# Adding the causal mask of a diagonal score block on VectorE in place of TensorE

## The chip, the cores and the metric

The kernel runs on one core of one Trainium2 chip. The time is the device time of one execution in microseconds, as the median of several runs. A profiled execution on the same core gives the trace from which all rows below are read. In the trace PE is TensorE's matmul side, PEld its weight load, DVE is VectorE, ACT is ScalarE, POOL is GpSimd and SP is SyncE.

## What is computed

The kernel computes one transformer layer on 2 x 1024 tokens of width 512: a token embedding from a hot and a cold table, a LayerNorm, causal attention with 16 heads of width 32, a residual sum, a second LayerNorm, and a mixture of 16 experts (2 per token) with a shared expert. The change touches the attention only. Cut to that:

```python
qkv = jnp.einsum('bsd,od->bso', x, w_project)            # b=2, s=1024, d=512
q, k, v = ...                                            # [b, 16 heads, s, 32]
att = jnp.einsum('bhqd,bhkd->bhqk', q, k) / math.sqrt(HEAD_DIM)
causal = jnp.triu(jnp.ones((s, s), dtype=bool), k=1)
att = jnp.where(causal[None, None, :, :], jnp.float32(-1e9), att)
att = jax.nn.softmax(att, axis=-1)
out = jnp.einsum('bhqk,bhkd->bhqd', att, v)
```

## The kernel before

The program has three stages that follow each other on each engine: the embedding (up to about 136 us of the span), the attention (136.5 to 634 us) and the output projection with the router and the experts (from 634 us). Each engine has an instruction stream written out by hand, and the streams meet only in semaphores.

The attention is cut into 8 **units**: a unit is one batch row b and one group of 4 heads, so that u = 2g + b. A unit has 32 **steps**, n = 0 to 31. Step n handles head h = n % 4 of the query tile i = n // 4, 128 query rows against (i + 1) * 128 keys. Units 1 to 6 run in a loop of three rounds of two units (`Fori`); units 0 and 7 are written out before and after it.

The order on TensorE within step n is: the scores of step n + 1 (`scores`, L492), the turning of the probabilities of step n - 1 (`turn`, L508), a piece of the projection of the next unit (`fill_piece`, L471, in four steps of five from n = 2 on, and not at all in unit 7, which has no next one), and in each step with n % 4 == 2 the product of the probabilities with V for the query tile before (`heads`, L519), followed by the transposition of the reciprocal sums (L531).

`scores` waits until ScalarE's exp of the step two before it is done (L495), because the scores of even and of odd steps share one pair of PSUM banks each. It multiplies with all keys up to the diagonal in pieces of up to 512 columns (L502). Into the piece that holds the diagonal block it then adds the mask with a second product, the identity times `mask_bf` in bf16 (L504), in the same accumulation. `s_S` is counted up behind the last product. Queries are stored with the negative scale, so the scores are negated, the mask is a large positive number above the diagonal, and the row maximum is taken as a minimum.

VectorE's step n (`unit`, L654) is: `row_max` of step n (L632, the reduction L638), in two or three steps of a unit the copy of a projected piece out of bank 7 (`fill_evac`, L460 and L469), the copy of the second half of the turned probabilities of step n - 2 (`copy_turned`, L584, only for i >= 4), the reciprocals of the sums when n % 4 == 0 (L644 and L646), and `normalize` when n % 4 == 3 (L652), which waits for ScalarE's `z_rows`.

ScalarE's step n is: the copy of the first half of the turned probabilities of step n - 2 (L582), the exp of step n with its row sums (L597), at times a projected piece (L456, L467), and the copy of `z_rows` when n % 4 == 3 (L604).

So a step's scores pass through this chain: TensorE scores, VectorE reduction, ScalarE exp, and from there to TensorE's turn of the same step and to the scores two steps on. VectorE's copies of turned probabilities set PSUM banks 4 and 5 free for later turns.

Of the kernel before, what the change touches and what calls it, by code (L numbers as in the profile page):

```python
# [16 lines left out]
ALU = mybir.AluOpType  # L17
# [3 lines left out]
P = 128  # L21
# [40 lines left out]
def build(nc, a, out):  # L62
    ctx = ExitStack()
    with ctx:
        def sb(name, shape, dt=F32, where=ctx):
            return where.enter_context(nc.sbuf_tensor(name, shape, dt))

        def sem(name):
            return ctx.enter_context(nc.semaphore(name))
# [3 lines left out]
        ident_bf = sb("ident_bf", [P, P], BF16)  # L73
        tri_bf = sb("tri_bf", [P, P], BF16)
        ones_bf = sb("ones_bf", [P, P], BF16)
        mask_bf = sb("mask_bf", [P, P], BF16)
# [11 lines left out]
        def bank(i, n=1):  # L88
            return psum[:, i:i + n, :].rearrange("p a n -> p (a n)")
# [64 lines left out]
        q_stack, k_stack, v_unit = [], [], []  # L154
# [139 lines left out]
        s_fdve = sem("projection_copied_by_dve")  # L294
# [2 lines left out]
        s_stack = [sem(f"stacks_loaded{b}") for b in range(BATCH)]  # L297
        s_S = sem("scores_ready")
        s_M = sem("row_max_ready")
        s_E = sem("probs_ready")  # L300
        s_T = sem("probs_turned")
        s_Ca = sem("probsT_copied_by_act")
        s_Cd = sem("probsT_copied_by_dve")
        s_Zr = sem("z_reciprocal_ready")
        s_Z = sem("z_inverse_ready")
        s_PV = sem("heads_summed")
        s_ZR = sem("z_rows_ready")
        s_AT = sem("attnT_ready")
# [42 lines left out]
        HEAD = 16  # L351
        STACKED = 16 * 8 * GH
        STEPS = QT * GH
        FILLS = 6

        def turned_banks(i):
            return 1 if i < 4 else 2
# [9 lines left out]
        def bank_no(i, h, k):  # L367
            return banks.index((i, h, k))

        def copies(e, upto):  # L370

            return sum(copier(*x) == e for x in banks[:upto])

        def wait_bank_free(pe, u, n):

            m = n - 2
            x = banks[m % UB]
            v = u if m >= 0 else u - 1
            e = copier(*x)
            pe.wait_ge(s_Ca if e == "act" else s_Cd, HEAD + v * UCOPY[e] + copies(e, m % UB + 1))  # L380
# [110 lines left out]
        def att_pe(pe):  # L491
            def scores(u, b, n):  # L492
                i, h = n // GH, n % GH

                pe.wait_ge(s_E, HEAD + u * STEPS + n - 1)  # L495
                dst = bank(2 * (n % 2), 2)
                qs = q_stack[b][:, h, i * P:(i + 1) * P]
                for c0 in range(0, (i + 1) * P, 512):

                    c1 = min(max((i + 1) * P, c0 + 256), c0 + 512)  # L500
                    own = c0 <= i * P < c1
                    mm = pe.matmul(dst[:, c0:c1], qs, k_stack[b][:, h, c0:c1], start=True, stop=not own)  # L502
                    if own:
                        mm = pe.matmul(dst[:, i * P:(i + 1) * P], ident_bf[:, :], mask_bf[:, :], start=False,  # L504
                                       stop=True)
                mm.then_inc(s_S, 1)

            def turn(u, n):  # L508
                i, h = n // GH, n % GH
                pe.wait_ge(s_E, HEAD + u * STEPS + n + 1)  # L510
                for k in range(turned_banks(i)):
                    m = bank_no(i, h, k)
                    wait_bank_free(pe, u, m)
                    for j in range(4 * k, min(4 * k + 4, i + 1)):
                        mm = pe.transpose(bank(4 + m % 2)[:, (j - 4 * k) * P:(j - 4 * k + 1) * P],  # L515
                                          probs[n % PSLOTS][:, j * P:(j + 1) * P], ident[:, :])
                    mm.then_inc(s_T, 1)

            def heads(u, b, i):  # L519

                last = bank_no(i, GH - 1, turned_banks(i) - 1) + 1
                for e, s in (("act", s_Ca), ("dve", s_Cd)):
                    pe.wait_ge(s, HEAD + u * UCOPY[e] + copies(e, last))

                pe.wait_ge(s_AT, HEAD + u * QT + i)
                for j in range(i + 1):
                    for h in range(GH):
                        pe.matmul(bank(6)[32 * h:32 * h + 32, 0:P], v_unit[b][:, j, 32 * h:32 * h + 32],  # L528
                                  probsT[i % 2][:, h, j * P:(j + 1) * P], start=(j == 0), stop=(j == i))
                pe.wait_ge(s_Z, HEAD + u * QT + i + 1)  # L530
                pe.transpose(bank(6)[:, P:2 * P], z_inv[:, i % 2, :, :].rearrange("p h d -> p (h d)"),  # L531
                             ident[:, :]).then_inc(s_PV, 1)

            def unit(u, b, g, prev, nxt):

                for n in range(STEPS):
                    if n + 1 < STEPS:
                        scores(u, b, n + 1)
                    elif nxt:
                        first_scores(u + 1, 1 - b, g + b)  # L540
                    if n >= 1:
                        turn(u, n - 1)
                    elif prev:
                        turn(u - 1, STEPS - 1)
                    if nxt and 0 <= (n - 2) // 5 < FILLS and (n - 2) % 5 < KC:
                        fill_piece(pe, u + 1, 1 - b, (n - 2) // 5, (n - 2) % 5, 16 * (g + 1 + b))
                    if n % GH == 2:
                        if n > GH:
                            heads(u, b, n // GH - 1)
                        elif prev:  # L550
                            heads(u - 1, 1 - b, QT - 1)

            def first_scores(u, b, g):

                pe.wait_ge(s_stack[b], STACKED * (g + 1))
                pe.wait_ge(s_fact, HEAD + 3 * u + 3)
                pe.wait_ge(s_fdve, HEAD + 3 * u + 3)
                scores(u, b, 0)

            first_scores(0, 0, 0)  # L560
            unit(0, 0, 0, False, True)
            with pe.Fori(0, GROUPS - 1) as g:
                unit(2 * g + 1, 1, g, True, True)
                unit(2 * g + 2, 0, g + 1, True, True)
            last = 2 * GROUPS - 1
            unit(last, 1, GROUPS - 1, True, False)
            turn(last, STEPS - 1)
            heads(last, 1, QT - 1)
# [62 lines left out]
        def att_dve(dve):  # L631
            def row_max(u, n):  # L632
                i = n // GH
                dve.wait_ge(s_S, HEAD + u * STEPS + n + 1)

                dve.wait_ge(s_E, HEAD + u * STEPS + n - 3)

                dve.tensor_reduce(nmax[:, n % 4:n % 4 + 1], bank(2 * (n % 2), 2)[:, 0:(i + 1) * P], AX.X,  # L638
                                  ALU.min).then_inc(s_M, 1)
# [832 lines left out]

        @block.vector
        def _(dve):
            for s in (s_M, s_Cd, s_Zr, s_Z, s_AT, s_fdve):
                dve.sem_inc(s, HEAD)
            step = Chain(dve, s_dve)
            dve.wait_ge(s_in, 32)
# [225 lines left out]
```

## Time and profile before

| what | value |
|---|---|
| median of 3 runs | 1120.07 us (1119.99 to 1125.67) |
| profiled execution, whole time | 1121.66 us |
| its span in the trace | 1119.7 us |
| TensorE's mean granted clock | 0.968 of full |
| busy: PE, PEld, DVE, ACT, POOL | 90%, 57%, 49%, 45%, 28% |
| attention, 136.5 to 634 us: busy PE, DVE, ACT | 476.2, 293.6, 351.1 of 497.5 us |

The profiled execution's span is 1119.7 us, and about 2 us lie around it (1121.66 in all). The busy shares are means over stages of different kinds. For a change in the attention, what counts is which engine or wait comes last in the attention, step by step, and that is read from the timeline and from the chain of waits.

### The profile page before, as it was taken

To read this page: it belongs to the slowest core of one execution; us is meant where nothing else is said; L and a number is where in the kernel's file an instruction comes from. 1 tells how busy PE (TensorE), PEld (TensorE's weight loads), DVE (VectorE), ACT (ScalarE), POOL (GpSimd) and SP (SyncE) were. 2 spreads that over 40 slices of the span, in tenths; PEclk is the share of its full clock that TensorE was granted. 3 is DMA by queue.
4 is the path that set the end of the run, shared out by engine and by line. 5 is a ranking of instruction groups with operands and counts; after the bars stand their busy time and mean duration, and the time that the engine had idled before them with its cause. 6 is when DMAs were issued, how large, how long until landed. Compare 5 with 4: busy or idle time off the path is not lost.

```text
span 1119.7 us, 22789 instructions
## 1 busy us (share of the span) xinstructions
PE 1003.6 (90%) x6879; PEld 638.8 (57%) x6880; DVE 551.2 (49%) x1422; ACT 499.1 (45%) x1195; POOL 319.0 (28%) x413
## 2 busy tenths in 40 slices
PE   5767699999989999899998899899898998799994
PEld 3323458676765858477676687778543444344441
DVE  7985347465645657365567677578311111111110
ACT  7512177676757777576778422111121222122221
POOL 1077220111102020110202046333144554445542
PEclk9779799999999999899999999899899999999997
DMA  5032733240513333050434111611296448744443
GB/s 199 30 84 84 177 77 79 70 109 11 135 40 76 78 76 87 26 136 13 105 96 144 61 73 57 263 47 48 93 286 186 85 91 239 232 91 84 85 87 43
DMA packets 44571, 114.35 MB, mean 102 GB/s; under 512 B 9332, under 2 KB 11380, under 8 KB 42162
## 3 DMA queue, kind: packets, MB, share of 16 engines
q1 hardware_dynamic: 32146, 87.14, 26.5%
q0 software_dynamic: 12320, 25.90, 12.1%
q8 instruction: 55, 0.90, 0.3%
q14 instruction: 50, 0.41, 0.1%
HBM read 53.03 MB, written 25.17 MB: 70 GB/s over the span
## 4 chain that ended last, share of the span: by engine, by line
PE 53%; DMA 19%; issue 11%; DVE 8%; POOL 4%; ACT 2%; POOLq 1%; DVEq 0%; ACTq 0%
DMA out<-y_sb,out_no 18%; PE psum L515 10%; PE psum L481 7%; PE psum L528 6%; PE psum L502 6%; PE psum L486 5%; PE psum L1200 4%; PE psum L1184 3%; PE psum L1256 2%; PE psum L531 1%; PE psum L504 1%; PE psum L1277 1%; DVE nmax L638 1%; DVE oh_lo L1497 1%; POOL hot_all L1422 1%
## 5 line engine op out<-in xcount | busy, mean ns | idle before, releaser
L638 DVE TENSOR_REDUCE nmax<-psum 128x1 f32<-128x128 f32 (+7 forms) x256 | 192.1, 753 | 79.9 <-PE psum L504 69.3
L597 ACT ACTIVATE probs<-psum,nmax 128x128 f32<-128x128 f32 (+7 forms) x256 | 190.7, 745 | 53.0 <-DVE nmax L638 47.7
L1256 PE MATMUL psum<-attnT,x_T 128*128 x376 | 182.8, 609 | 9.5 <-issue 8.2
L502 PE MATMUL psum<-k_stack,q_stack 128*128 128x512 f32 (+2 forms) x384 | 157.2, 464 | 24.4 <-issue 15.3
L515 PE MATMUL psum<-ident,probs 128*128 128x128 f32 x1152 | 174.9, 278 | 3.8 <-DVE probsT L584 1.4
L1157 DVE COPY x_T<-psum 128x512 f32<-128x512 f32 x47 | 32.5, 692 | 249.8 <-PE psum L1299 249.8
L582 ACT COPY probsT<-psum 128x512 f32<-128x512 f32 (+3 forms) x256 | 129.1, 504 | 55.2 <-PE psum L515 43.5
L481 PE MATMUL psum<-xnT,w_unit 128*128 128x512 f32 x256 | 131.4, 603 | 0.2 <-ACT full L456 0.2
L515 PEld LDWEIGHTS psum<-ident,probs 128*128 128x128 f32 x1152 | 124.5, 142 | 9.1 <-DVE probsT L584 3.8
L428 POOL CAST part_hi<-full 128x512 fp32r<-128x512 f32 x32 | 19.6, 613 | 375.6 <-ACT full L456 267.7
L1256 PEld LDWEIGHTS psum<-attnT,x_T 128*128 128x128 f32 x376 | 66.1, 193 | 87.5 <-issue 87.1
L502 PEld LDWEIGHTS psum<-k_stack,q_stack 128*128 128x128 f32 x384 | 69.1, 202 | 67.0 <-ACT probs L597 33.2
L1335 PE MATMUL psum<-w_dn,gated_T 128*128 x188 | 88.5, 593 | 1.0 <-ACT gated_T L909 1.0
L850 POOL DMA_INDIRECT out<-y_sb,out_no x47 | 75.4, 1604 | 44.4 <-POOL out_no L847 44.4
L940 ACT ACTIVATE y_sb<-psum,slot_w 128x512 f32<-128x512 f32 x47 | 32.3, 687 | 104.3 <-PE psum L1335 100.4
L528 PE MATMUL psum<-probsT,v_unit 128*32 128x128 f32 x2304 | 77.1, 278 | 0.8 <-ACT probsT L582 0.8
L528 PEld LDWEIGHTS psum<-probsT,v_unit 128*32 128x32 f32 x2304 | 59.8, 111 | 27.7 <-ACT probsT L582 19.4
L652 DVE TENSOR_TENSOR attnT<-psum,z_rows 128x128 f32 (+1 forms) x64 | 18.7, 291 | 114.8 <-ACT z_rows L604 114.8
L486 PE MATMUL psum<-w_unit,xnT 128*128 128x128 f32 x512 | 66.7, 275 | 0.3 <-DVE full L460 0.3
L584 DVE COPY probsT<-psum 128x128 f32<-128x128 f32 (+3 forms) x128 | 61.6, 481 | 2.7 <-PE psum L515 2.5
L836 POOL DMA_INDIRECT x_rows<-xn_scratch,rows_no x47 | 50.0, 1065 | 42.5 <-POOL rows_no L833 36.1
L486 PEld LDWEIGHTS psum<-w_unit,xnT 128*128 128x128 f32 x512 | 61.7, 192 | 0.5 <-issue 0.5
(222 smaller groups left out, 1489.3 us busy)
## 6 DMA issues: line engine op xcount, KB each, us to landing
attnT<-in_wgu SPq DMA_DIRECT2D x16, 1024.0 KB, 5.0
q_stack<-part_hi SPq DMA_DIRECT2D x64, 128.0 KB, 2.4
q_stack<-part_lo SPq DMA_DIRECT2D x64, 128.0 KB, 2.4
k_stack<-part_hi SPq DMA_DIRECT2D x64, 128.0 KB, 2.4
k_stack<-part_lo SPq DMA_DIRECT2D x64, 128.0 KB, 2.6
w_dn<-in_wd SPq DMA_DIRECT2D x16, 512.0 KB, 6.2
out<-acc SPq DMA_DIRECT2D x17, 256.0 KB, 2.1
hot_all<-xn SPq DMA_DIRECT2D x4, 1024.0 KB, 8.3
```

The source lines that it names most:

```text
L481: mm = pe.matmul(bank(7), w_unit[:, k, side * P:(side + 1) * P], xnT[:, k, t0:t0 + 512], start=(k == 0), stop=(k == KC - 1), skip_group_ch ...
L486: mm = pe.matmul(bank(7)[:, k * P:(k + 1) * P], xnT[:, c, t0:t0 + P], w_unit[:, c, 2 * P:3 * P], start=(c == 0), stop=(c == KC - 1))
L502: mm = pe.matmul(dst[:, c0:c1], qs, k_stack[b][:, h, c0:c1], start=True, stop=not own)
L515: mm = pe.transpose(bank(4 + m % 2)[:, (j - 4 * k) * P:(j - 4 * k + 1) * P], probs[n % PSLOTS][:, j * P:(j + 1) * P], ident[:, :])
L528: pe.matmul(bank(6)[32 * h:32 * h + 32, 0:P], v_unit[b][:, j, 32 * h:32 * h + 32], probsT[i % 2][:, h, j * P:(j + 1) * P], start=(j == 0), ...
L582: eng.copy(dst, src).then_inc(s_Ca, 1)
L584: eng.tensor_copy(dst, src).then_inc(s_Cd, 1)
L597: act.activation(probs[n % PSLOTS][:, 0:(i + 1) * P], bank(2 * (n % 2), 2)[:, 0:(i + 1) * P], ACT.Exp, bias=nmax[:, n % 4:n % 4 + 1], scal ...
L638: dve.tensor_reduce(nmax[:, n % 4:n % 4 + 1], bank(2 * (n % 2), 2)[:, 0:(i + 1) * P], AX.X, ALU.min).then_inc(s_M, 1)
L850: pool.indirect_dma_start(out=out, out_offset=bass.IndirectOffsetOnAxis(ap=out_no[s][:, :], axis=0), in_=y_sb[:, s, :], in_offset=None, bo ...
L1256: mm = pe.matmul(bank(2 + p), lhs(k), rhs(k), start=(k == 0), stop=(k == KC - 1), skip_group_check=True)
L1335: mm = pe.matmul(bank(6 + p), gated_T[:, p, k * P:(k + 1) * P], w_dn[:, bass.ds(half, 1), k, :].rearrange("p o n -> p (o n)"), start=(k == 0),
```

## The change

`scores` issues the score products alone, and each of them closes its accumulation. `row_max` has a new instruction ahead of the reduction: VectorE adds `mask_bf` (bf16 in SBUF) in place to the 128 x 128 diagonal block of the scores in PSUM, counts up a new semaphore `s_masked`, and waits for it before it reduces. This is done in all 256 steps. The new semaphore starts at `HEAD` like the others.

```diff
@@ att_pe / scores @@
-                    own = c0 <= i * P < c1
-                    mm = pe.matmul(dst[:, c0:c1], qs, k_stack[b][:, h, c0:c1], start=True, stop=not own)
-                    if own:
-                        mm = pe.matmul(dst[:, i * P:(i + 1) * P], ident_bf[:, :], mask_bf[:, :], start=False,
-                                       stop=True)
+                    mm = pe.matmul(dst[:, c0:c1], qs, k_stack[b][:, h, c0:c1], start=True, stop=True)
                 mm.then_inc(s_S, 1)
@@ att_dve / row_max @@
                 dve.wait_ge(s_S, HEAD + u * STEPS + n + 1)
                 dve.wait_ge(s_E, HEAD + u * STEPS + n - 3)
+                own = bank(2 * (n % 2), 2)[:, i * P:(i + 1) * P]
+                dve.tensor_tensor(own, own, mask_bf[:, :], ALU.add).then_inc(s_masked, 1)
+                dve.wait_ge(s_masked, HEAD + u * STEPS + n + 1)
                 dve.tensor_reduce(nmax[:, n % 4:n % 4 + 1], bank(2 * (n % 2), 2)[:, 0:(i + 1) * P], AX.X,
                                   ALU.min).then_inc(s_M, 1)
@@ block.vector @@
-            for s in (s_M, s_Cd, s_Zr, s_Z, s_AT, s_fdve):
+            for s in (s_M, s_masked, s_Cd, s_Zr, s_Z, s_AT, s_fdve):
                 dve.sem_inc(s, HEAD)
```

## Rows read from the trace of the kernel before

**Rows 1.** The page's part 1: busy time, share, instructions of each engine.

```profile
PE 1003.6 (90%) x6879; PEld 638.8 (57%) x6880; DVE 551.2 (49%) x1422; ACT 499.1 (45%) x1195; POOL 319.0 (28%) x413
```

**Rows 2.** Busy time by stretch: a unit inside the loop, then the last unit.

```profile
core 0: us, PE busy (x) PEld busy (x) DVE busy (x) ACT busy (x) POOL busy (x), PEclk, DMA share, GB/s
199.00:263.00 64.00, 63.32 (x653) 44.73 (x656) 37.81 (x78) 45.66 (x115) 7.53 (x8) 1.00 0.29 67
...
582.00:634.00 52.00, 43.31 (x535) 31.21 (x523) 34.47 (x70) 40.05 (x97) 7.43 (x8) 1.00 0.29 103
```

**Rows 3.** Groups by line: shapes xcount | busy us, mean ns | idle before, releasers.

```profile
L638 DVE TENSOR_REDUCE nmax<-psum 128x1 f32<-128x128 f32 (+7 forms) x256 | 192.1, 753 | 79.9 <-PE psum L504 69.3 <-issue 7.7
...
L504 PE MATMUL psum<-mask_bf,ident_bf 128*128 128x128 bf16 x256 | 59.7, 233 | 0.0
```

**Rows 4.** Timeline of PE around step 29 of unit 1: start, duration, instruction.

```profile
251.53 0.23 PE L504 MATMUL psum<-mask_bf,ident_bf 128*128 128x128 bf16 x1
251.60 1.04 PE L515 MATMUL psum<-ident,probs 128*128 128x128 f32 x8
...
253.83 0.23 PE L504 MATMUL psum<-mask_bf,ident_bf 128*128 128x128 bf16 x1
```

**Rows 5.** Timeline around steps 7 and 8 of unit 1, DVE, ACT, PE.

```profile
206.89 0.43 DVE L638 TENSOR_REDUCE nmax<-psum 128x1 f32<-128x256 f32 x1 [0.85 <-PE psum L504]
...
207.53 0.49 ACT L597 ACTIVATE probs<-psum,nmax 128x256 f32<-128x256 f32 x1
...
208.42 0.29 DVE L652 TENSOR_TENSOR attnT<-psum,z_rows 128x128 f32 x1 [1.10 <-ACT z_rows L604]
...
208.63 0.55 DVE L638 TENSOR_REDUCE nmax<-psum 128x1 f32<-128x384 f32 x1
...
209.09 0.17 DVE L644 RECIPROCAL z_rec<-z_sum 128x4 f32<-128x4 f32 x1
...
209.29 0.32 DVE L646 COPY z_inv<-z_rec 128x128 f32<-128x128 f32 x1
...
209.69 0.19 ACT L597 ACTIVATION_READ_ACCUMULATOR probs<-psum,nmax 128x1 f32 x1
...
209.93 0.60 PE L502 MATMUL psum<-k_stack,q_stack 128*128 128x384 f32 x1
```

**Rows 6.** Timeline around step 12 of unit 1.

```profile
214.73 0.68 DVE L638 TENSOR_REDUCE nmax<-psum 128x1 f32<-128x512 f32 x1
...
216.27 0.19 PEld L502 LDWEIGHTS psum<-k_stack,q_stack 128*128 128x128 f32 x1 [0.90 <-ACT probs L597]
```

**Rows 7.** Timeline around steps 16 to 19 of unit 1.

```profile
222.67 0.69 DVE L460 COPY full<-psum 128x512 f32<-128x512 f32 x1 [0.41 <-PE psum L481]
...
223.65 1.56 DVE L638 TENSOR_REDUCE nmax<-psum 128x1 f32<-128x640 f32 x2
...
225.44 0.30 PEld L502 LDWEIGHTS psum<-k_stack,q_stack 128*128 128x128 f32 x2 [0.93 <-ACT probs L597]
```

**Rows 8.** Timeline around step 21 of unit 1.

```profile
232.68 0.69 DVE L460 COPY full<-psum 128x512 f32<-128x512 f32 x1 [0.54 <-PE psum L481]
...
233.62 0.44 PE L515 MATMUL psum<-ident,probs 128*128 128x128 f32 x2 [0.20 <-DVE probsT L584]
```

**Rows 9.** Timeline around steps 1 to 3 of unit 2.

```profile
260.32 0.37 ACT L597 ACTIVATE probs<-psum,nmax 128x128 f32<-128x128 f32 x1
...
260.83 0.19 PEld L502 LDWEIGHTS psum<-k_stack,q_stack 128*128 128x128 f32 x1 [0.17 <-ACT probs L597]
```

**Rows 10.** Timeline of DVE, steps 29 and 30 of unit 1.

```profile
250.74 0.55 DVE L584 COPY probsT<-psum 128x384 f32<-128x384 f32 x1
251.80 1.22 DVE L638 TENSOR_REDUCE nmax<-psum 128x1 f32<-128x1024 f32 x1 [0.51 <-PE psum L504]
```

**Rows 11.** Busy time by stretch, query tile 6 of the last unit (columns as in Rows 2).

```profile
610.80:618.50 7.70, 7.21 (x88) 5.36 (x87) 6.33 (x11) 6.57 (x14) 0.00 (x0) 1.00 0.01 2
```

**Rows 12.** The chain that ended last: start, duration, what; the loop's return.

```profile
319.74 3.80 issue
```

More of the change, by code:

```diff
@@ L299, in build @@
         s_M = sem("row_max_ready")
+        s_masked = sem("own_block_masked")
         s_E = sem("probs_ready")
```

## Prediction

> **What bounds the kernel now.** I read the page's engine totals first: TensorE is busy for 90% of the span, VectorE for 49% [rows 1]. That says little for one stage, so the second view is the busy time by stretch. In a unit inside the loop (64 us) TensorE is busy for 63.3 us and VectorE for 37.8; in the last unit, which has no projection pieces to fill gaps, TensorE falls to 43.3 of 52 us, while VectorE keeps 34.5 [rows 2]. So units 0 to 6 are bound by TensorE, with short waits, and unit 7 by the loop of scores, reduction, exp and next scores. The third view, the groups by line, gives 256 mask products and 256 reductions; most of VectorE's idle time ahead of a reduction ends with the mask product [rows 3]. That is VectorE waiting for scores, and not yet a cost. The fourth view, the timeline, shows where TensorE in turn waits for what comes from the reduction [rows 5 to 9].
>
> **What the change takes away.** A mask product is recorded with 233 ns [rows 3], but products overlap and the recorded ends are modelled. What it holds TensorE for is the distance to the next start: L504 starts at 251.53, the first L515 at 251.60, so 0.07 us [rows 4]. Its weight load lies in the same 0.07. The most it can give is 256 x 0.07 = 17.9 us. The same 0.07 goes from each step's latency, as VectorE can start when the last score product ends. The risk below that: without the small product the weight load of the first turned block stands directly behind L502. It then lies beside a product of 256 columns or more instead of one of 128, so I see no reason for a new bubble; the gain per product lies between 0 and 0.08 us and I take 0.07.
>
> **What it adds.** One VectorE addition of 128 x 128 in each of the 256 steps, with one operand in PSUM, and the reduction waits for its end. The trace has no addition that reads and writes PSUM. The nearest row is L652, a TENSOR_TENSOR of the same size out of PSUM: 0.29 us [rows 5]. For a dependent pair the nearest rows are L644, 0.17 us long, and L646, which waits for it and starts 0.20 us after it, so 0.03 behind its end [rows 5]. That makes 0.32 us from the start of the addition to the start of the reduction, and I take it, since it is the sum of the two nearest rows. The lower end is the distance at which an independent instruction follows L652, 208.42 to 208.63, so 0.21 us [rows 5]. As upper end I estimate 0.45: the two spacings of 0.21 and 0.20 one behind the other, and a little for the write into PSUM, which no row has. A gain is excluded, since the addition is new work ahead of an unchanged reduction. Nothing of this is TensorE's, and no DMA moves.
>
> The Trainium skill, page "VectorE: DVE Perf Modes", section "The DRAIN you can't avoid", says that a semaphore between VectorE instructions costs nothing extra, since the next waits for the pipeline in any case. Here L638 starts 0.08 us before L652's recorded end, and L646 only 0.03 after L644's, so the trace speaks against it for a dependent pair [rows 5]. By the rule the mask would cost 0.21 us; this is a rival below.
>
> **Where the 0.32 is hidden.** Behind the addition on VectorE stand the reduction, the copies of turned probabilities, the fill copies and the reciprocals. In the late query tiles of a loop unit there is room: VectorE is idle for 0.51 us ahead of the reduction at 251.80 [rows 10], and the heads product fills TensorE once per four steps. So for tiles 6 and 7 I cost it at nothing. If that cover goes, each step pays what the addition exceeds it by.
>
> **Where it isn't hidden, loop units.** Five places per unit bound TensorE by a chain:
> - Step 8: exp of step 7 starts at 207.53, z_rows and L652 (208.42) follow, then the reduction of step 8, the exp that ends 209.88, and the scores at 209.93, which had no slack [rows 5]. The addition of step 7 pushes that exp by about 0.15 (its minimum was ready at 207.32 and a hand-over takes 0.04), that of step 8 by 0.32: +0.47.
> - Step 12: L638 at 214.73, then its exp, scores at 216.27, held by the exp [rows 6]: +0.32.
> - Steps 16 to 19: the fill copy at 222.67 starts when TensorE's piece ends, then come two reductions from 223.65 on, the exp, and scores at 225.44, held by the exp [rows 7]: +0.32, once for the three steps, as the second chain starts from the same fill copy.
> - Step 21: the fill copy at 232.68 waits for TensorE, the turn at 233.62 for the copy behind it [rows 8]. No addition lies between, and the one before ends in the 0.54 us of idle time: 0.
> - Change of unit: the exp at 260.32, whose minimum a later reduction would make late, then the scores at 260.83 [rows 9]: +0.32.
>
> Together +1.43 us. Nine mask products lie within these stretches, whose length the chain sets, so their 0.07 is not gained. The other 23 give 23 x 0.07 = 1.61 us. Net -0.18 per unit; units 0 to 6 have this pattern seven times: -1.3 us. For smaller waits that don't exist yet I add 0.1 per unit, an allowance without a row: +0.7.
>
> **Last unit.** Without fill pieces each query tile passes two reductions in the chain (tile start, and two steps on). Per tile +2 x 0.32 - 0.07 = 0.57 us, for tiles 1 to 7: +4.0 us; tile 0 is in the change of unit. VectorE's own load agrees: in tile 6 it is busy for 6.33 of 7.70 us [rows 11], and four additions of 0.32 make 7.61.
>
> **Sum.** -1.3 + 0.7 + 4.0 = +3.4 us. The profiled execution would go from a span of 1119.7 to 1123.1, with the same 2 us around it to 1125.1. The median before is 1120.07, 1.6 below the profiled one, so the median after is 1120.07 + 3.4 = 1123.5 us. Outside the attention nothing changes.
>
> With 0.21 instead of 0.32, the places of a unit give 0.21 x 4 + 0.04 = 0.88, the unit -0.73, the last unit 7 x 0.35 = 2.5, the sum -5.1 + 0.7 + 2.5 = -1.9: 1118.2 us. With 0.45: 4 x 0.45 + 0.28 = 2.08, the unit +0.47, seven +3.3, last unit 7 x 0.83 = 5.8, with 0.7 in all +9.8: 1129.9 us.
>
> **Rivals.**
> 1. *TensorE's gain is kept.* The chains absorb the addition in units 0 to 6, since TensorE's idle time there is 0.7 us of 64 [rows 2] and most of that could be the same wait. Then 7 x 32 x 0.07 = 15.7 us come off and only the last unit pays 4.0: -11.7, 1108.4 us. With half the places absorbing, about 1115. Against it: at step 8 the scores start 0.05 us behind the exp's end, and at steps 12 and 16 the exp is named as what held them [rows 5 to 7].
> 2. *The semaphore is free* (the rule above): 1118.2 us, as worked out.
> 3. *VectorE becomes the bound in late tiles of the loop units* (slower). The place is tile 7: per step a reduction of 1.22 and a copy of 0.55 to 0.68, less overlaps, make about 1.75 [rows 10]; with 0.32 it is 2.07 against TensorE's 2.30 a step (251.53 to 253.83) less 0.07 [rows 4]. It decides from an addition of 0.5 us on. At 0.6 the excess is 0.1 over 8 steps of 7 units, 5.6 us, and the five places give 7 x 1.1 more: about 1137 us. For it speaks that tile 7 has stretches without a gap; against, the 0.51 us of idle time [rows 10].
> 4. *Instruction supply.* At the loop's return all engines stand for 3.80 us [rows 12]. VectorE's stream grows by one instruction a step and TensorE's shrinks by two. If this puts one more pause of 1 to 2 us into each of the three rounds, the sum is +3.4 + 4.5: 1128 us. The Trainium skill, page "Runtime: NRT & Kernel Launch", section "Instruction fetch mechanics", says that a taken branch outside the loaded blocks forces a fetch; the trace agrees with such a pause at the return, and a longer body could add one.
> 5. *The change doesn't shorten TensorE's path*, since a weight load takes the mask product's place: the 1.61 of each unit is missing, +3.4 + 11.3: 1134.8 us.
>
> **Chances.** Forecast with 0.32 (1120 to 1128): 0.50. Rival 1: 0.14. Rival 2: 0.08. Rival 3: 0.12. Rival 4: 0.11. Rival 5: 0.05. What can be told from no change here is about 0.5%, 5.6 us, so faster is below 1114.5 and slower above 1125.7. Faster takes 0.09 of rival 1. Slower takes 0.13 of the forecast's upper part, all of rivals 3 and 5 and 0.09 of rival 4: 0.39. The rest, 0.52, is no change. The range 1115 to 1132 leaves out rival 1 but for its upper part, half of rival 3, and rival 5.
>
> **What the changed profile would show.** The mask addition at 0.29 us and the reduction starting 0.32 after it; L515 starting 0.07 earlier behind the scores; a loop unit within 0.5 us of its old length with longer waits of L502 for the exp; the last unit 4 us longer, VectorE near full in tiles 5 to 7. It would be wrong if additions take over 0.4 us, if loop units move by over 1 us, or if pauses of instruction supply differ.

## The result

The changed kernel takes 1128.49 us in the median of 9 runs (1126.54 to 1130.49), beside 1120.07 us before (9 runs, 1118.32 to 1125.67) on the same chip. The ratio is 1.0066, with a 95% interval of 1.0047 to 1.0085: slower by 7.4 us (5.3 to 9.5). The forecast was 1123.5 us with a range of 1115 to 1132.

The changed kernel's profiled execution spans 1126.4 us, beside 1119.7. Its totals on the page answer to [rows 1], and its busy time by stretch (unit 1, then the last unit) to [rows 2]:

```profile
PE 999.8 (89%) x6623; PEld 643.8 (57%) x6624; DVE 620.9 (55%) x1678; ACT 493.5 (44%) x1195; POOL 318.6 (28%) x413
```

```profile
core 0: us, PE busy (x) PEld busy (x) DVE busy (x) ACT busy (x) POOL busy (x), PEclk, DMA share, GB/s
198.00:262.00 64.00, 61.41 (x592) 44.22 (x596) 46.91 (x112) 44.69 (x114) 7.54 (x8) 1.00 0.30 68
584.60:636.60 52.00, 43.31 (x422) 30.76 (x418) 40.63 (x93) 39.29 (x94) 7.34 (x8) 0.90 0.29 103
```

VectorE has 256 instructions more and TensorE 256 products fewer. In 64 us of unit 1 TensorE is busy for 1.9 us less. From landmark to landmark (the measure by query tile below) its busy time in the unit fell from 60.75 to 59.95 us while the unit grew from 61.36 to 62.10, so 1.5 us more are waits. In the last unit TensorE's granted clock has fallen to a mean of 0.90, where it was 1.00; more on that below.

The groups by line, as in [rows 3]. ScalarE's idle time ahead of the exp, which ends with the reduction, is 93.7 us, where it was 47.7. The first row is that of the kernel before:

```profile
L597 ACT ACTIVATE probs<-psum,nmax 128x128 f32<-128x128 f32 (+7 forms) x256 | 190.7, 745 | 53.0 <-DVE nmax L638 47.7
```

```profile
L594 ACT ACTIVATE probs<-psum,nmax 128x128 f32<-128x128 f32 (+7 forms) x256 | 190.2, 743 | 97.1 <-DVE nmax L638 93.7
L638 DVE TENSOR_REDUCE nmax<-psum 128x1 f32<-128x128 f32 (+7 forms) x256 | 194.0, 758 | 8.8
...
L635 DVE TENSOR_TENSOR psum<-psum,mask_bf 128x128 f32<-128x128 f32 x256 | 75.5, 295 | 37.2 <-PE psum L502 27.7
```

The timeline of a query tile's start (step 4 of unit 3): the addition takes 0.29 us and the reduction starts 0.33 us behind its start, 0.04 after its end.

```profile
332.46 0.29 DVE L652 TENSOR_TENSOR attnT<-psum,z_rows 128x128 f32 x1 [3.49 <-ACT z_rows L601]
...
332.67 0.29 DVE L635 TENSOR_TENSOR psum<-psum,mask_bf 128x128 f32<-128x128 f32 x1
333.00 0.42 DVE L638 TENSOR_REDUCE nmax<-psum 128x1 f32<-128x256 f32 x1
```

The waits of TensorE's weight loads over one unit (columns: who <- for whom: us in total, times, longest), first before, 199 to 262 us, then after, 199 to 262 us:

```profile
PEld psum L502 <- ACT probs L597: 3.3, 7, 0.9
...
PEld psum L515 <- DVE probsT L584: 0.4, 1, 0.4
```

```profile
PEld psum L502 <- ACT probs L594: 7.4, 11, 1.4
...
PEld psum L512 <- DVE probsT L581: 1.1, 4, 0.5
```

The scores' wait for the exp has grown from 7 places to 11, and a second wait, for VectorE's copies, from 1 place to 4.

**A measure by query tile.** The attention's streams are the same in each execution, so the start of L531 (the transposition of the reciprocal sums, once per query tile) is a clean landmark in each trace. The stretch "tile t" below is the time from one such start to the next in which the scores of tile t are issued; "tile 0" is the one over the change of unit. The table shows each stretch's difference from the kernel before, in us, for unit 1; its rows are named after the experiments below. Units 3 and 5 agree with it within 0.04. Units 2, 4 and 6, the second half of the loop's body, differ in single tiles by pauses that are told of below, and their last stretch holds the loop's return. In the changed kernel tile 5 is 0.50 longer there and tile 7 0.07 to 0.09 longer:

```
kernel        tile 1  tile 2  tile 3  tile 4  tile 5  tile 6  tile 7  tile 0    unit
changed        -0.07   +0.21   +0.24   +0.26   +0.18   -0.31   -0.11   +0.34   +0.74
no_mask        -0.30   -0.24   -0.15   -0.08   -0.16   -0.31   -0.31   -0.08   -1.63
both           +0.08   +0.33   +0.34   +0.33   +0.33    0.00    0.00   +0.40   +1.81
indep          +0.01   +0.06   +0.22   +0.58   +0.19    0.00    0.00   +0.29   +1.35
tile67          0.00    0.00   +0.01    0.00   -0.01   -0.30   -0.11   +0.01   -0.40
third_step     -0.08   -0.08   -0.07   -0.01   +0.33   -0.31   -0.11    0.00   -0.33
third_fourth   -0.14   -0.15   -0.08   -0.01   +0.33   -0.31   -0.10   +0.09   -0.37
only22         +0.01    0.00   +0.01    0.00   +0.32    0.00    0.00    0.00   +0.34
swap22          0.00    0.00   +0.01    0.00   -0.12   +0.02    0.00    0.00   -0.09
starts         +0.09   +0.18   +0.35   -0.08   +0.35    0.00    0.00   +0.08   +0.97
picked         -0.15   -0.14    0.00    0.00   -0.01   -0.30   -0.11    0.00   -0.71
```

From the first such start to the output projection's first product the kernel before takes 488.5 us and the changed one 497.3: 8.8 us more. The span grew by 6.7, as the parts ahead of and behind it came out 2 us shorter in that execution. Behind the attention a kernel's stretch lay between 484.5 and 492.7 us over all traces, with nothing changed in it (the kernels ran on several chips), so single spans don't tell these kernels apart; ratios over several runs and the attention's own time do.

### The profile page after: what moved, and what is told of

It is laid out like the page before. It is cut to its first block, busy times and chain, and to the rows that moved or that the text cites. A ratio compares the mean times of both kernels' runs of the same rounds, so it can differ in the third digit from the quotient of the medians.

```text
span 1126.4 us, 22534 instructions
## 1 busy us (share of the span) xinstructions
PE 999.8 (89%) x6623; PEld 643.8 (57%) x6624; DVE 620.9 (55%) x1678; ACT 493.5 (44%) x1195; POOL 318.6 (28%) x413
## 4 chain that ended last, share of the span: by engine, by line
PE 46%; DMA 19%; issue 13%; DVE 12%; POOL 4%; ACT 4%; POOLq 1%; ACTq 0%; DVEq 0%
DMA out<-y_sb,out_no 19%; PE psum L512 8%; PE psum L482 6%; PE psum L525 5%; PE psum L502 5%; PE psum L487 5%; PE psum L1200 4%; PE psum L1184 3%; DVE nmax L638 3%; PE psum L1256 2%; PE psum L1277 2%; DVE psum L635 2%; ACT probs L594 1%; POOL hot_all L1422 1%; PE psum L528 1%
## 5 line engine op out<-in xcount | busy, mean ns | idle before, releaser
L594 ACT ACTIVATE probs<-psum,nmax 128x128 f32<-128x128 f32 (+7 forms) x256 | 190.2, 743 | 97.1 <-DVE nmax L638 93.7
L512 PE MATMUL psum<-ident,probs 128*128 128x128 f32 x1152 | 180.1, 279 | 4.5 <-DVE probsT L581 2.4
L502 PE MATMUL psum<-k_stack,q_stack 128*128 128x512 f32 (+2 forms) x384 | 153.1, 454 | 34.2 <-ACT probs L594 21.5
L512 PEld LDWEIGHTS psum<-ident,probs 128*128 128x128 f32 x1152 | 137.5, 142 | 40.5 <-issue 15.2
L635 DVE TENSOR_TENSOR psum<-psum,mask_bf 128x128 f32<-128x128 f32 x256 | 75.5, 295 | 37.2 <-PE psum L502 27.7
L581 DVE COPY probsT<-psum 128x128 f32<-128x128 f32 (+3 forms) x128 | 61.6, 481 | 2.1 <-PE psum L512 2.1
```

Of the source, the lines that this page charges most:

```text
L594: act.activation(probs[n % PSLOTS][:, 0:(i + 1) * P], bank(2 * (n % 2), 2)[:, 0:(i + 1) * P], ACT.Exp, bias=nmax[:, n % 4:n % 4 + 1], scal ...
L635: dve.tensor_tensor(own, own, mask_bf[:, :], ALU.add).then_inc(s_masked, 1)
```

## The experiments

### TensorE's gain by itself

The changed kernel without its addition, so no causal mask in the diagonal block at all:

```diff
-                own = bank(2 * (n % 2), 2)[:, i * P:(i + 1) * P]
-                dve.tensor_tensor(own, own, mask_bf[:, :], ALU.add).then_inc(s_masked, 1)
-                dve.wait_ge(s_masked, HEAD + u * STEPS + n + 1)
```

> This kernel leaves the causal mask of the diagonal block out altogether: no product on TensorE, no addition on VectorE. It shows TensorE's gain by itself. Theory 1 (a product holds TensorE for 0.07 us, in units 0 to 6 nearly all of it comes off, in the last unit a part): 16 us faster than before, 12 to 18. Theory 2 (a weight load takes the product's place, so that TensorE gains nothing): within 2 us of before.

Measured: ratio 0.9879 (0.9848 to 0.9909) to the kernel before, 13.6 us faster. Unit 1 is 1.63 us shorter, tiles 1, 6 and 7 by 0.30 to 0.31 each: four products of 0.07 with 0.03 over. In the other tiles less comes off, as there the chain of waits sets a part of the stretch. The last unit is 1.5 us shorter, but 0.97 of it has nothing to do with the products: it is in tile 3, where one VectorE copy took 1.24 us in the kernel before and 0.35 here (the account of the last unit, below, shows it). So theory 1 holds, and the gain per loop unit is the 1.61 that the prediction had.

### VectorE's cost by itself

The kernel before with the addition put in (the wait is shown in the changed kernel's form, which comes to the same count):

```diff
                     mm = pe.matmul(dst[:, c0:c1], qs, k_stack[b][:, h, c0:c1], start=True, stop=not own)
                     if own:
                         mm = pe.matmul(dst[:, i * P:(i + 1) * P], ident_bf[:, :], mask_bf[:, :], start=False,
                                        stop=True)
 ...
+                dve.tensor_tensor(own, own, mask_bf[:, :], ALU.add).then_inc(s_masked, 1)
+                dve.wait_ge(s_masked, HEAD + u * STEPS + n + 1)
```

> The product on TensorE is kept as before, and VectorE's addition with its semaphore is there too, so the mask is added twice (the probabilities stay the same). It shows VectorE's cost by itself. Theory 1 (each place where TensorE waits for a chain through a reduction grows by 0.32 us per addition in the chain, 7 to 8 such per loop unit and 2 per query tile of the last): 21 us slower than before, 17 to 24. Theory 2 (the places are only the five of the prediction): 7 x 1.43 + 4.5 = 14.5 us slower. Theory 3 (the addition is hidden, and what made the change slow is on TensorE): under 8 us slower.

Measured: ratio 1.0131 (1.01 to 1.0163), 14.8 us slower. The tiles show the pattern plainly: tiles 2 to 5 grow by 0.33 each, that is by one addition per query tile; tiles 6 and 7 by nothing; the change of unit by 0.48 (tiles 0 and 1). One unit costs 1.81, and the last unit 5.65. The size is that of theory 2 (14.5), but by luck. The units alone come to 7 x 1.81 + 5.65 = 18.3 us, within the 17 to 24 of theory 1; the trace's attention is 15.5 us longer, as the pause at the loop's return was about 3 us shorter in it. The places fit neither theory: there is one addition's worth in each of the tiles 2 to 5, where the prediction had 0.47, 0.32, 0.32 and nothing, and 0.48 at the change of unit, where it had 0.32. Theory 1 had 7 to 8 additions that count in a loop unit, and there are between 5 and 6.

### The same addition, with nothing waiting for it

```diff
-                dve.tensor_tensor(own, own, mask_bf[:, :], ALU.add).then_inc(s_masked, 1)
-                dve.wait_ge(s_masked, HEAD + u * STEPS + n + 1)
+                dve.wait_ge(s_masked, HEAD + u * STEPS + n)
+                dve.tensor_tensor(spare[:, :], own, mask_bf[:, :], ALU.add).then_inc(s_masked, 1)
```

> The product on TensorE is kept as before. VectorE makes an addition of the same size out of the same scores, but writes it to a spare tile in SBUF, and the reduction does not wait for it. Against the kernel with both, this takes away the wait for the end of the addition and the write to PSUM. Theory 1 (an addition that nothing waits for takes 0.21 us of VectorE, one that the reduction waits for 0.32): two thirds of the cost of both, 14 us slower than before. Theory 2 (a semaphore between two VectorE instructions costs nothing): the same as both, about 21 us slower.

Measured: ratio 1.0068 (1.0043 to 1.0093), 7.7 us slower, half of what `both` cost and less than either theory had. Two of its timeline rows, and the same place in the changed kernel (step 29 of unit 1 in each):

```profile
249.73 0.29 DVE L652 TENSOR_TENSOR spare<-psum,mask_bf 128x128 f32<-128x128 f32 x1
249.94 1.21 DVE L654 TENSOR_REDUCE nmax<-psum 128x1 f32<-128x1024 f32 x1
```

```profile
249.34 0.30 DVE L635 TENSOR_TENSOR psum<-psum,mask_bf 128x128 f32<-128x128 f32 x1
249.68 1.22 DVE L638 TENSOR_REDUCE nmax<-psum 128x1 f32<-128x1024 f32 x1
```

The addition is as long in both. With nothing waiting, the reduction starts 0.21 us after it, while its last 0.08 us still run; with the wait, 0.34 after. Tiles 3 and 5 grow by 0.22 and 0.19 instead of 0.34 and 0.33. The kernel differs from `both` in where it writes as well as in the wait, so 0.13 us is the price of the two together. The Trainium skill, page "VectorE: DVE Perf Modes", section "The DRAIN you can't avoid", says that a semaphore between VectorE instructions costs nothing extra, because the next one waits for the pipeline in any case. Here the trace disagrees with the reason: without the semaphore the reduction starts 0.08 us before the addition's recorded end. What the semaphore costs alone, with the same destination, no run here shows.

Tile 4 with +0.58 is more than an addition explains. In units 2, 4 and 6 it is +0.22 to +0.23, and in unit 1 the chain through it has 0.40 us, at 221.92, in which VectorE waits for nothing that the profile shows: one of the pauses told of below.

### The addition only where it gained

In query tiles 6 and 7 of units 0 to 6; elsewhere the product (`on_pe` is the complement of `on_dve`, and the last unit has the product):

```diff
+        def on_dve(last, n):
+            return not last and n >= 24
 ...
+                if on_dve(is_last(u, n), n):
                     dve.tensor_tensor(own, own, mask_bf[:, :], ALU.add).then_inc(s_masked, 1)
```

> VectorE adds the mask only in query tiles 6 and 7 of units 0 to 6 (8 of 32 steps); all other steps, and the last unit, have the product on TensorE as before. By the two traces the stretch with tile 6 is 0.30 us shorter per unit after the change, and that with tile 7 between 0.11 shorter and 0.07 longer. Theory 1 (these tiles have the room on VectorE, and the loss is elsewhere): 7 x 0.3 to 0.4, 2 to 3 us faster than before, ratio 0.9975. Theory 2 (every place with an addition loses): 1 us slower or more.

Measured: ratio 0.9948 (0.9927 to 0.9969), faster. In units 1, 3 and 5 tile 6 comes out 0.30 and tile 7 0.11 shorter, and all others are unmoved: 0.40 us per unit (in unit 0 both gain 0.30). In units 2, 4 and 6 tile 7 is 0.42 longer instead, with a pause of 0.24 us on VectorE at its start, and nothing is gained there. So theory 1 holds for the stretches, and the edit's own work is some 1.5 us. The interval of the ratio reaches from 3.5 to 8.2, and the attention of its trace is 5.2 us shorter: 2.6 of that is a shorter pause at the loop's return, and 1.1 lies in the last unit, which has the products as before. The ratio has a large part that is not the edit's own work.

### The last unit without the addition

```diff
+        def on_dve(last, n):
+            return not last
```

> The changed kernel, but in the last unit (from its step 1 on) the product on TensorE is back and VectorE adds nothing. Theory 1 (the last unit lost 5.1 us to the additions in its chain and to a stretch of 10 us at half the TensorE clock that came with the longer waits): the last unit is back at its length before, 5 us less than the changed kernel's, its clock stays at 1.0, and the loop units keep their loss of 0.7 us each. Against before 2 to 4 us slower. Theory 2 (the half clock comes from the DMA burst in that unit): the half clock stays, the last unit is 1 to 1.5 us above before.

Measured: ratio 1.0029 (1.0006 to 1.0052). The last unit is back at 49.36 us (before 49.67, changed kernel 54.81); its clock stays at 1.00, though the transfers in it run as before. Units 1, 3 and 5 keep their 0.70 to 0.71. So theory 1 holds: the last unit's 5.1 us are the additions' work and what follows from them.

### TensorE kept busy in the last unit

The changed kernel, with idle products in the last unit:

```diff
                 for n in range(STEPS):
+                    if is_last(u, n) and n in WARM:          # {5: 8, 6: 3, 9: 5}
+                        for _ in range(WARM[n]):
+                            pe.matmul(bank(7)[:, 0:P], ident[:, :], ident[:, :], start=True, stop=True)
                     if n + 1 < STEPS:
                         scores(u, b, n + 1)
```

> The changed kernel, with idle products added in the last unit only: 8, 3 and 5 products of the identity with itself (0.11 us each) into a free PSUM bank, ahead of the scores of steps 6, 7 and 10, where TensorE waits for the exp anyway. Theory 1 (the clock fell to half since TensorE was busy for only 2.2 of 4.1 us): the granted clock stays at 1.0 and the last unit is 1 to 1.5 us shorter than in the changed kernel, though TensorE does more. Theory 2 (the clock does not hang on these gaps): it falls as before, the last unit keeps its 54.8 us or is longer.

Measured: ratio 1.0065 (1.0041 to 1.0088). Busy time by stretch from the last unit's start on, 4.1 us and then 8 us, for the kernel before, the changed one, and this one:

```profile
582.52:586.62 4.10, 3.10 (x31) 2.06 (x28) 2.11 (x7) 3.22 (x13) 0.00 (x0) 1.00 0.62 214
586.62:594.62 8.00, 5.77 (x50) 3.57 (x48) 5.71 (x13) 6.17 (x21) 6.47 (x8) 1.00 1.03 389
```

```profile
584.62:588.72 4.10, 2.22 (x23) 1.46 (x19) 2.95 (x11) 2.65 (x11) 0.00 (x0) 1.00 0.64 222
588.72:596.72 8.00, 6.67 (x43) 4.44 (x36) 4.88 (x13) 5.19 (x17) 6.48 (x8) 0.51 1.03 388
```

```profile
585.68:589.78 4.10, 4.10 (x45) 3.86 (x41) 2.90 (x11) 2.61 (x11) 0.00 (x0) 1.00 0.64 212
589.78:597.78 8.00, 6.37 (x58) 4.58 (x50) 5.68 (x15) 5.47 (x19) 6.50 (x8) 1.00 1.03 388
```

In the changed kernel TensorE was busy for 2.22 of 4.1 us, and the granted clock then fell from 1.00 to 0.51, the 1.2 GHz level. With the 8 and 3 idle products in the same stretch it is busy throughout, and the clock stays at 2.4 GHz (1.00), with the same transfers beside it. So the fall hangs on TensorE's idle time, and theory 2 is out. The last unit goes from 54.81 to 54.21 us, 0.6 and not 1 to 1.5. That is what is left after the idle products' own cost: each of them is recorded as two, and the first 8 take 1.7 us, twice the 0.11 each that was expected. The whole kernel's ratio can't tell 0.6 us apart.

The additions are not the only way into this: in `only22` below the last unit is as before, and its clock fell too, to 0.50 from 599.70 to 603.10 us, behind 4.1 us in which TensorE was busy for 2.11.

### One more step of four, and two more

```diff
+            return not last and (n >= 24 or n % 4 == 2)        # third_step
+            return not last and (n >= 24 or n % 4 >= 2)        # third_fourth
```

> VectorE adds the mask in query tiles 6 and 7 and, in tiles 0 to 5, in every third of four steps (n % 4 == 2), whose exp has the heads product to hide behind; units 0 to 6 only. All other steps and the last unit have the product on TensorE. Theory 1 (only the additions at a tile's start, n % 4 == 0, and those before them on VectorE lose; the rest gains 0.07 us a step outside the chains): each loop unit 0.6 to 0.8 us shorter than before, 0.3 more than with tiles 6 and 7 alone, 5 us in all. Theory 2 (every addition in tiles 1 to 5 pushes the next tile's start): about 0, or slower.

> As the kernel before this one, with the additions in steps n % 4 == 3 as well. The exp of such a step stands right ahead of the copy of z_rows on ScalarE, which starts the chain of the next tile. Theory 1 (that exp has some slack, 0.17 us at step 7, so 0.15 of 0.32 is passed on): each loop unit between 0.4 and 0.9 us shorter than before, so no better than the third step alone by more than 0.2. Theory 2 (what isn't at a tile's start is free): 1.0 us shorter each.

Measured: 0.9967 (0.9944 to 0.999) and 0.996 (0.9941 to 0.998). The third steps gain 0.08 each in tiles 1 to 3, nothing in tile 4, and tile 5 grows by 0.33, which eats all of it. The fourth steps gain 0.06 more in tiles 1 and 2, and cost 0.09 at the change of unit. So a loop unit is 0.33 and 0.37 us shorter, against forecasts of 0.6 to 0.8 and 0.4 to 0.9, and no better than with tiles 6 and 7 alone. Neither theory for the third step gave the one tile that loses.

### What is late in tile 5

One addition alone, in step 22; and the same with VectorE's order turned round in that step:

```diff
+            return not last and n == 22                        # only22, swap22
 ...
-                    row_max(u, n)
+                    if n != 22:
+                        row_max(u, n)
 ...
                         copy_turned(dve, "dve", u, n - 2)
+                        if n == 22:                            # swap22 alone
+                            row_max(u, n)
```

> As before the change, but step 22 of units 0 to 6 (tile 5) has VectorE's addition in place of the product. Theory 1 (VectorE's copy of the turned block of step 20 stands behind row_max of step 22, and TensorE's turn of step 21 waits for that copy to free its bank): the stretch between the transpositions of the sums of tiles 3 and 4 grows by 0.32 us in each of these units, all others stay within 0.03. Theory 2 (the loss of that stretch comes from the chain through the reduction at the tile's start): no growth with this one addition, or 0.07 less.

> As the kernel before this one, and in step 22 of every unit VectorE makes its copy of the turned block ahead of row_max. Theory 1: the growth of 0.32 us is gone, the stretch is at its length before the change or up to 0.1 below; the later exp of step 22 is hidden by the heads product. Theory 2 (the addition costs there by another way): the growth stays, or gets larger by the 0.33 of the copy.

Both kernels, and the next, were timed once (1135.0 and 1128.5 us, and 1140.1, beside a median of 1128.7 before); single times differ by more than these effects, so the traces' stretches are what counts.

Measured: tile 5 grows by 0.32 to 0.34 in all seven units with the one addition, and with the order turned round it is 0.12 shorter than before in all seven. Tiles 6 and 7 move by 0.04 at most. (In units 2, 4 and 6 tile 3 is 0.35 longer in both kernels, by a pause told of below.) The timeline of the kernel before, of the one addition, and of the turned order, unit 1:

```profile
234.32 0.94 PE L515 MATMUL psum<-ident,probs 128*128 128x128 f32 x6
234.35 0.41 DVE L584 COPY probsT<-psum 128x256 f32<-128x256 f32 x1
```

```profile
234.33 0.28 DVE L596 COPY probsT<-psum 128x128 f32<-128x128 f32 x1
234.53 0.29 DVE L651 TENSOR_TENSOR psum<-psum,mask_bf 128x128 f32<-128x128 f32 x1
...
234.85 0.96 DVE L654 TENSOR_REDUCE nmax<-psum 128x1 f32<-128x768 f32 x1
235.36 0.60 PE L527 MATMUL psum<-ident,probs 128*128 128x128 f32 x4
235.73 0.41 DVE L596 COPY probsT<-psum 128x256 f32<-128x256 f32 x1
...
236.20 0.44 PE L527 MATMUL psum<-ident,probs 128*128 128x128 f32 x2 [0.23 <-DVE probsT L596]
```

```profile
233.08 0.42 DVE L596 COPY probsT<-psum 128x256 f32<-128x256 f32 x1 [0.53 <-PE psum L527]
...
233.31 0.82 PE L527 MATMUL psum<-ident,probs 128*128 128x128 f32 x6
```

With the one addition the turn of step 21 is cut in two: four blocks at 235.36, and two that wait until VectorE has copied the turned block of step 20 out of their bank. That copy stands behind the addition and the reduction in VectorE's queue. Before the change the six blocks ran in one go, and with the copy first they do again. So this loss has nothing to do with the row minimum being late. It comes from what is queued behind the addition.

### The addition at the tiles' starts

```diff
+            return not last and n in (0, 4, 8, 12, 16)         # starts
```

> As before the change, but steps 0, 4, 8, 12 and 16 of units 0 to 6 have VectorE's addition in place of the product. Theory 1 (one addition per query tile, the one at the tile's start, lies in the chain from z_rows to the exp that the scores two steps on wait for): the stretches of tiles 2, 3 and 4 grow by 0.25 to 0.4 us each, the change of unit and tile 1 by 0.1 to 0.4 together, tiles 5 to 7 stay: 1.0 to 1.4 us per unit. Theory 2 (the loss needs two additions in a row): under 0.5 us per unit.

Measured, unit 1: tile 3 grows by 0.35 and tile 2 by 0.18 (0.51 to 0.54 in units 2, 4 and 6), but tile 4 is 0.08 shorter, and the change of unit (tiles 1 and 0) 0.17 longer; in all 0.97, with a 0.35 in tile 5 that no addition stands in. That last one appears only in units 1, 3 and 5, and a like one in tile 2 only in units 2, 4 and 6, which points to the pauses below. So the start of a tile is the place in tile 3 and half of tile 2, and not in tile 4: there the start alone costs nothing, and all four together cost 0.33. The chain of tile 4 of the changed kernel runs through two additions, those of steps 16 and 17, with a wait of the scores for the exp between them that the kernel before does not have:

```profile
220.79 0.29 DVE L635 TENSOR_TENSOR psum<-psum,mask_bf 128x128 f32<-128x128 f32 x1
...
222.91 0.30 PEld L502 LDWEIGHTS psum<-k_stack,q_stack 128*128 128x128 f32 x2 [0.57 <-ACT probs L594]
...
222.91 0.30 DVE L635 TENSOR_TENSOR psum<-psum,mask_bf 128x128 f32<-128x128 f32 x1
```

Of the 0.97 us in unit 1 the additions explain 0.62, without the 0.35 in tile 5. That is between theory 1 (1.0 to 1.4) and theory 2 (under 0.5), and tile 4 goes against theory 1.

### The steps that gain, together

```diff
+            return not last and (n >= 24 or n in (2, 6, 7, 10, 11, 14))
```

> VectorE adds the mask in units 0 to 6 in query tiles 6 and 7 and in steps 2, 6, 7, 10, 11 and 14; all other steps and the last unit have the product on TensorE. These are the steps whose stretches got shorter in the runs so far. Theory 1 (gains of stretches add up, the additions of other steps don't come into them): each loop unit 0.7 to 0.9 us shorter than before, 5 to 6 us in all, ratio 0.995. Theory 2 (the gains interact): no better than tiles 6 and 7 alone, 0.3 to 0.4 us per unit.

Measured: ratio 0.9922 (0.9901 to 0.9943). This kernel is faster than the one before by 0.8%, and so than the changed one, which was slower than it. Units 1, 3 and 5 are 0.70 to 0.72 shorter, as theory 1 has it; of the tiles 1 to 3 the third gave nothing. Seven times 0.7 would be 4.9 us of the 8.8 that the ratio says. Its trace has the attention, from the first landmark on, 6.8 us shorter, but 2.7 of that lie at the loop's return, and in units 2, 4 and 6 tile 7 is 0.08 longer instead of 0.11 shorter. The rest is not explained by its additions: expected was a ratio of 0.995, and the interval ends at 0.9943.

## Why the prediction came out as it did

The measured 1128.5 lies in the range. But the case held likeliest, no change, had 0.52, "slower" had 0.39, and the forecast was too low by 5 us in the median and by 4 in the ratio. That the time stayed in the range owes something to luck: the places in the loop units and the last unit cost 8 us more than the sum had, and a shorter pause at the loop's return and one VectorE copy hid 3.7 of them. Of the signs by which it would be wrong, the pauses did differ; a loop unit was to stay within 0.5 us of its length, and unit 1 moved by 0.74.

- **TensorE's gain, right.** 23 x 0.07 = 1.61 us per loop unit was the forecast, and without any mask a unit is 1.63 shorter. Rival 5 is out.
- **The addition's price, right.** 0.32 us from addition to reduction was taken, and 0.33 is read. The prediction took it from a pair of rows that was not an addition in PSUM [rows 5].
- **The places in loop units, the step that failed.** The sum of five places was +1.43 us. Measured against the kernel with no mask, unit 1 grew by 2.37. By tile (changed less `no_mask`): tile 2 has 0.45 (step 8: forecast 0.47) and tile 3 0.39 (step 12: 0.32), right in size. That tile 2's part comes from the additions of steps 7 and 8 as forecast isn't shown: step 7's alone costs nothing (`third_fourth`, `picked`: -0.15), step 8's alone 0.18 (`starts`), and `both` has 0.33 there. Tile 4 has 0.34 where 0.32 was forecast, but by another chain: the forecast let it start at the fill copy [rows 7] with one addition in it, and it runs through the additions of steps 16 and 17 and gives a part of them back. That the two sizes agree is luck. Tile 5 has 0.34, where the prediction said nothing: it checked the addition ahead of the fill copy of step 21 [rows 8], found it hidden, which it is, and did not follow the addition of the step after to the copy queued behind it. The change of unit (tiles 0 and 1) has 0.42 + 0.23 where 0.32 was forecast; which additions make it up was not taken apart. Tile 7 has 0.20, where it was costed at nothing because of 0.51 us of idle time [rows 10]: in the changed kernel that gap is gone, and a turn waits 0.20 us for a copy (251.42 us, L512 for L581). The missing 0.94 us seven times is 6.6 us; the allowance of 0.1 per unit covered 0.7 of it.
- **Tile 6, right**: fully hidden, -0.31.
- **The last unit, right in kind and too small.** +4.0 was forecast and 5.1 measured. Tiles 1 and 4 to 7 grew by 0.59 to 0.69 each (forecast 0.57). The surplus lies in tiles 2 and 3, +1.96 together instead of 1.14, and it is larger than that looks. Tile 2 grew by 2.45 and tile 3 shrank by 0.49. In tile 3 the kernel before loses 1 us that the changed one doesn't, to a VectorE copy that stands beside a GpSimd instruction and ends 0.08 us behind it:

```profile
592.42 1.27 POOL L780 TENSOR_TENSOR wo_lo<-acc,wo_hi 128x512 fp32r<-128x512 f32 x1
592.53 1.24 DVE L646 COPY z_inv<-z_rec 128x128 f32<-128x128 f32 x1
```

  The same copy takes 0.23 us in the changed kernel (597.94), which meets the collision in tile 2 instead (591.09, 0.86 us). With that 1 us counted the additions and what follows from them cost about 6.1 us in the last unit, 2.1 more than forecast. By `warm` 0.6 net of it is the clock; how the rest divides between the additions and the longer copy in tile 2 was not taken apart.
- **Instruction supply (rival 4), small and real.** No pause was added at the loop's return. But in units 2, 4 and 6 of the changed kernel VectorE stands still for 0.24 us at the start of tile 5, waiting for nothing that the profile shows, and tile 5 is 0.32 longer there than in unit 1 (the row is of unit 2):

```profile
291.00 0.29 DVE L652 TENSOR_TENSOR attnT<-psum,z_rows 128x128 f32 x1 [1.88 <-ACT z_rows L601]
...
291.54 0.30 DVE L635 TENSOR_TENSOR psum<-psum,mask_bf 128x128 f32<-128x128 f32 x1 [0.24 <-issue]
```

  That is 1.0 us in three units; tile 7 is 0.18 longer there too, 0.5 in all, by a cause that was not looked for. The pauses at the loop's return [rows 12] differ by 2 us and more between kernels, in both directions. In the changed kernel's trace the three stretches with the return are 1.7 us shorter in all, where the change of unit should make them 1.0 longer, so the pauses took 2.7 us off.
- **The sum.** Forecast 3.4, plus 6.6 - 0.7 for the places, 1.5 for tiles 5 and 7 in units 2, 4 and 6, 1.1 for the last unit, less 2.7 at the loop's return: 9.2. The attention has 8.8 from the first landmark on, which leaves out the start of unit 0. The loop units' sign turned: net -0.18 was forecast, +0.74 measured.
- **Rival 1** (the gain is kept) held for tile 6 and for a third of tile 7's; **rival 2** (a free semaphore) is out by the 0.33; **rival 3** had the right cause, VectorE's queue, with the wrong place: VectorE does not become the bound of a whole tile, it is late for one copy. Its 1137 us also leaves out the last unit, where an addition of 0.6 instead of 0.32 would cost 7 x 0.56 = 3.9 us more.

## What to carry to other kernels

An instruction added on an engine off the critical path has two prices: the result that it delays, and everything that is queued behind it on that engine. For each step write down both, and who waits for the second: here it was a copy that frees a PSUM bank. Moving that one copy ahead took the whole 0.32 us away and 0.12 more, of which 0.07 is the product that TensorE no longer has.

Work can be moved between engines step by step. With the mask on VectorE in 14 of 32 steps of units 0 to 6 and on TensorE in the rest, the kernel gets 0.8% faster, of which 0.4% is traced to the steps, while moving all of it makes it 0.7% slower. The difference by tile in one trace of the full change showed where tiles 6 and 7 gained; which steps of tiles 1 to 3 to keep took further kernels.

## What the runs showed of the hardware

- The addition in place in PSUM that the reduction waits for costs 0.33 to 0.34 us from start to start, and the one into SBUF that nothing waits for 0.21, both being 0.29 long.
- TensorE's clock fell to 1.2 GHz (granted 0.51) behind 4.1 us in which it was busy for 2.22, and stayed at 2.4 GHz behind 3.10 and behind 4.10 of 4.1. A longer chain of waits can so slow down even what is not waiting; here keeping the clock up won 0.6 us net.
- In the loop, pauses in which VectorE waits for nothing that the profile shows sit at fixed places of the body. Adding or taking away instructions moves them: 0.3 to 0.5 us in each second unit, in a tile that depends on the kernel (tile 2, 3, 4, 5 or 7). That they are the supply of instructions is argued from this; no run measured the supply itself.
- VectorE's copy of the reciprocal sums (SBUF to SBUF, 0.23 us) is lengthened, up to 1.31 us (`only22`, 596.94), when it starts beside a GpSimd TENSOR_TENSOR, and then ends 0.08 to 0.09 us behind it. That is so for 166 such copies in the 14 traces; 10 others beside one stayed under 0.26 us. Which of the two meets the other moves with the timing, and in the last unit it is worth 1 us, a seventh of what the change costs. The critical chain calls this time "issue", so a pause should be looked up in the timeline before it is called one.
